# Moving the second batch's tap mixing from all four blocks of the first batch's convolution to the last three

## The reference

```python
logits = (x @ Wl.T + bl).reshape(Bq, Tq, H, K)
w = softmax(where(valid, logits, -inf), axis=-1)
y = einsum('bthk,btkhd->bthd', w, xg)
z = conv(y + bias, Wc) + bc
h = selu(z) @ W2.T + b2
```

## Time and profile before

| what | value |
|---|---|
| median of three runs | 1567.8 us (1564.4 to 1570.6) |
| the profiled execution, its own time | 1562.6 us |
| its span in the trace | 1560.8 us |
| TensorE (PE) busy | 1471.8 us, 94% |
| VectorE (DVE) busy | 1027.2 us, 66% |
| ScalarE (ACT) busy | 722.9 us, 46% |
| GpSimd (POOL) busy | 576.7 us, 37% |
| batch 0's convolution | from 48 to about 157 us of the span |

### The profile page before, as it was taken

How to read it: one execution, slowest core, us unless ns; L and a number is a source line. 1 busy time by engine, 2 the same in 40 slices (tenths; PEclk the granted TensorE clock), 3 DMA queues, 4 the chain that set the end, 5 groups by cost and what they waited for, 6 DMA issues and landing times.

```text
span 1560.8 us, 30456 instructions
## 1 busy us (share of the span) xinstructions
PE 1471.8 (94%) x11724; PEld 990.5 (63%) x11724; DVE 1027.2 (66%) x1973; ACT 722.9 (46%) x1272; POOL 576.7 (37%) x632
## 2 busy tenths in 40 slices
PE   2799999999999899999999999999999999999998
PEld 2456766766666677777777777778875444444444
DVE  2754434655566667677877787755647877876766
ACT  1331222122111255566655556557665665555654
POOL 2220001001101478603460237002995564555655
PEclk9999999999999999999999999999999999999999
DMA  7441110110000278703260225000233443344543
GB/s 192 111 130 31 24 35 18 31 34 21 22 21 28 71 159 187 172 2 63 62 164 6 64 62 136 6 20 2 84 90 111 120 142 110 120 137 117 151 129 107
DMA packets 143906, 128.47 MB, mean 82 GB/s; under 512 B 86970, under 2 KB 124306, under 8 KB 142738
## 3 DMA queue, kind: packets, MB, share of 16 engines
q1 hardware_dynamic: 127186, 110.65, 27.0%
q0 software_dynamic: 2272, 12.06, 2.5%
q10 hardware_dynamic: 14304, 3.81, 1.3%
HBM read 106.24 MB, written 5.28 MB: 71 GB/s over the span
## 4 chain that ended last, share of the span: by engine, by line
PE 66%; POOL 11%; DVE 9%; DMA 6%; ACT 3%; issue 2%; SPq 2%; POOLq 0%; DVEq 0%; ACTq 0%
PE ps L1729 6%; PE ps L1731 5%; PE ps L1730 5%; PE ps L1995 5%; PE ps L1996 5%; PE ps L1997 5%; PE ps L1937 3%; PE ps L1931 3%; PE ps L1932 3%; DMA region_k<-region_c 3%; PE ps L1866 3%; PE ps L1901 2%; PE ps L1890 2%; PE ps L1896 2%; PE ps L1891 2%; PE ps L2007 2%
## 5 line engine op out<-in xcount | busy, mean ns | idle before, releaser
L992 ACT ACTIVATE region_c<-ps 128x720 f16<-128x720 f32 (+1 forms) x228 | 175.3, 769 | 232.8 <-PE ps L1901 232.8
L859 POOL TENSOR_TENSOR region_k<-region_c,region_k 128x480 f16<-128x480 f32 x198 | 216.8, 1096 | 164.8 <-ACT region_k L1113 164.6
L1353 DVE TENSOR_TENSOR region_c<-ps,region_c 128x720 f16<-128x720 f32 (+1 forms) x228 | 205.9, 903 | 96.8 <-ACT ps L993 94.6
L1729 PE MATMUL ps<-region_k 128*128 128x360 f16 (+1 forms) x752 | 240.7, 320 | 2.7 <-DVE region_k L1182 2.7
L1730 PE MATMUL ps<-region_k 128*128 128x360 f16 (+1 forms) x752 | 239.8, 319 | 0.0
L1731 PE MATMUL ps<-region_k 128*128 128x360 f16 (+1 forms) x752 | 239.8, 319 | 0.0
L1358 DVE TENSOR_REDUCE region_c<-ps 120x1 f32<-120x512 f32 x252 | 173.3, 688 | 75.4 <-PE ps L1866 72.9
L1931 PE MATMUL ps<-region_k,region_c 128*120 128x129 f16 (+1 forms) x1368 | 179.0, 220 | 1.9 <-ACT region_c L992 1.9
L1932 PE MATMUL ps<-region_k,region_c 128*120 128x128 f16 (+1 forms) x1368 | 178.1, 219 | 0.0
L993 ACT ACTIVATE ps<-ps 128x720 f32<-128x720 f32 (+1 forms) x228 | 174.6, 766 | 0.0
L743 POOL TENSOR_TENSOR vare<-mv,eps 120x6 f32<-120x6 f32 x20 | 3.9, 197 | 452.0 <-DVE mv L1261 452.0
(11 more groups left out here) (275 smaller groups left out, 2725.0 us busy)
## 6 DMA issues: line engine op xcount, KB each, us to landing
gates<-gates_dram SPq DMA_DIRECT2D x384, 120.0 KB, 2.8
region_c<-in_k SPq DMA_DIRECT2D x56, 256.0 KB, 2.9
region_c<-in_v SPq DMA_DIRECT2D x56, 256.0 KB, 3.1
region_c<-in_WcT POOLq DMA_DIRECT2D x8, 1024.0 KB, 6.2
region_c<-in_experts SPq DMA_DIRECT2D x18, 352.0 KB, 3.0
gates<-band_dram SPq DMA_DIRECT2D x26, 189.0 KB
region_c<-in_k POOLq DMA_DIRECT2D x14, 256.0 KB, 3.0
region_k<-region_c SPq DMA_TRANSPOSE x120, 3.1
```

What stands on the lines that cost most here:

```text
L859: g.tensor_tensor(a_lo[u], ac[u], a_hi[u], ALU.subtract).then_inc(s["a_lo_ready"], 1)
L992: a.activation(halves(p_hi[u][0:parts]), st, ACT.Exp).then_inc(s["p_hi_ready"], 1)
L1353: v.tensor_tensor(halves(p_lo[u][0:parts]), two(2 * u, parts), halves(p_hi[u][0:parts]), ALU.subtract).then_inc(s["lo_ready"], 1)
L1729: mm(o, wh[:, m, j], xh[:, j:j + w], start=(j == 0), stop=False)
```

## The change

Batch 1's mixing, done during batch 0's convolution, is spread over quarters 12 to 45 and not 1 to 43. The mixing of batches 2 and 3, the attention steps and the weights' steps stay in their quarters.

```diff
-MIX_SPAN, ATTN_SPAN = (1, 43), (3, 48)
+MIX_SPAN, FIRST_SPAN, ATTN_SPAN = (1, 43), (12, 45), (3, 48)
...
-    for row, (first, last) in ((mix, MIX_SPAN), (down + attn, ATTN_SPAN)):
+    for row, (first, last) in ((mix, MIX_SPAN if b else FIRST_SPAN), (down + attn, ATTN_SPAN)):
```

## The result

In 21 runs each the changed kernel had a median of 1572.3 us and the kernel before 1569.4 us; the ratio is 1.0026 (95% interval 1.0017 to 1.0036), which is 4.1 us slower (2.7 to 5.6). The three estimates are 4.1, 6.9 and 3.9 us, on the mean 5.0 us or 0.3%; each interval lies clear of no change. The profiled execution took 1575.0 us, its span 1573.2.

What follows compares the result with a forecast made beforehand. TensorE was taken to bound the kernel; -9.0 + 9.6 + 3.1 + 3.9 = +7.6 us on the profiled 1562.6 gives 1570.2, and 5.2 more for the median gives 1575.4 us, range 1565 to 1580.

Steps and rivals of the forecast that it cites:

- what the prediction put at nothing: Split moved to quarter 43, batch 2's x load, weights' steps, second band write, later windows' reads: no cost to TensorE.
- What the change takes away: Batch 0's convolution: wait at logits 1 (3.1), slow clock behind it (3.1), old band 0 wait (2.8) go; 9.0 us.
- The walk to taps 1: VectorE's moved chain from quarter 12 at 71.6 us through logits, low 4 and sums 4, ending taps 1 at 91.8.
- rival 3: VectorE, relieved of backlog, has taps 1 ready by 82.2, so no band 0 wait: -5.1 us, 1562.7; chance 0.08.
- The hold in line 1155: In logits 1, GpSimd's addition set off by low 4 holds this VectorE instruction, 2.65 us over its usual 0.28.
- The wait at band 0: TensorE at quarter 21 waits 9.6 us for the band's 10.5 us way through DRAM after taps 1; bounds 7.8 to 10.9.
- rival 4: Piece 7's load shares DMA engines with band write and reads, 3 us more: wait 13, sum +11, 1579; chance 0.06.
- The slow clock behind it: After the long band 0 wait the granted clock drops, costing TensorE 3.1 us; ends 2 and 3.5.
- The short waits: Bank 3, TensorE waiting for VectorE's apply reads: band 4 2.6, band 1 1.1, apply 5 0.2; sum 3.9 us.
- The sum: Whole kernel: -9.0 + 9.6 + 3.1 + 3.9 = +7.6 us, 0.48% slower; terms' ends +3.3 to +10.4.
- What a measurement can tell: Whole-kernel timing: about 0.5% (7.8 us) is what a measurement can tell from no change.

Runs made afterwards that it cites:

- Experiment 4: Changed kernel with batch 1's eight band windows packed from quarter 25 to 42: ratio to before 0.9961; the same with logits and taps back at 1, 2, 4, 6: 0.9972.
- experiment 2: Kernel before, with logits 1 of batch 1 put into free bank 5 so TensorE need not wait there: ratio 0.9991.
- experiment 6: Changed kernel, high 5 behind taps 1, low 4, sums 4, low 5 in quarter 20: ratio 1.0014; with apply 0 and 3 earlier 0.9984; with late windows 0.9970.
- second and third comparison: The unedited changed kernel timed twice more against the kernel before: ratios 1.0044 and 1.0025.
- experiments 5: Changed kernel with low 4, sums 4 and high 5 moved behind taps 1, quarter 16: ratio to before 1.0035; with apply 0 and 3 one quarter earlier 0.9996.

## Why the prediction was right, and where it was too large

- **Direction and mechanism: right.** The change made the kernel slower, by a wait at band 0 that takes the place of two smaller ones. Experiment 4 shows it from the other side: give the transport four more quarters and the loss turns into a gain. No other wait of TensorE shows in the changed kernel between 47 and 180 us, save those counted below, so what the prediction put at nothing cost nothing.
- **What the change takes away (9.0 us): right as a count of what the profile held.** Both waits are gone in the profiles. But it was read as TensorE's own loss, and experiment 2 shows that it was VectorE's: a wait taken from logits 1 comes back at the product reads. The late place of the logits did relieve VectorE, so the 9 us went in the changed kernel; experiment 4 puts the worth of that move, once the windows are late, at 1.7 us only, net of the 2.5 us that late logits still left at band 0.
- **The walk to taps 1: right to 0.1 us once its start is allowed for.** Forecast 91.8 with quarter 12 at 71.6; measured 89.95, in an execution that started 1.4 us earlier and had its full clock sooner, with logits 0 read from 73.97 where 75.8 was forecast: both are 1.8 earlier. VectorE was not just in time for logits 0, as forecast, but idle for 1.24 us ahead of it; that changed nothing, since TensorE set the start. (In rival 3 the four pieces of VectorE's work called 7.8 us add up to 7.0 by the durations given; nothing hangs on it.) The hold in line 1155 was forecast at 2.93 and was 2.93. By the Trainium skill's rule (SBUF — State Buffer, "SBUF: two separate sides") this instruction, begun at 79.60 and so 0.42 us ahead of the addition at 80.02, would have got through; the trace again doesn't agree for that instruction.
- **The wait at band 0 (9.6 us): 11.7, 9.9 and 10.2.** The two last are within 0.6, partly by luck: the write was quicker than the 7.17 assumed and the read slower. The write took 8.4 us in the first profile and 6.0 and 6.3 in the others, having 5.4 to 8.5. Piece 7's load was issued 2.6 us behind it in all three, so the load doesn't explain the 8.4, and nothing here does. The read took 3.6, 4.2 and 4.2 us where the earlier trace rows had 2.76; that load was still under way beside it, and experiment 6 shows what loads beside the read cost. So rival 4, given 0.06, was in part a feature of every execution and not a case of its own, but the whole way was only 0.3 to 2.1 us longer than 10.5, not 3.
- **The slow clock behind it (3.1 us): about right in the profiles, and incomplete.** Take away the waits and the slow clock, and the stretch of before is 110.8 - 9.0 = 101.8. The changed kernel's three stretches less their waits are 105.3, 105.6 and 103.4: 3.5, 3.8 and 1.6 us of slow clock. In the first two it fell a second time, behind band 4's wait of 2.6 us, which I hadn't foreseen, since 2.8 us had not brought it down before; in the third the same wait left it at 1.00.
- **The short waits (1.1, 2.6, 0.2): 1.19, 2.59 and none.**
- **The sum: too large.** +7.6 us against +4.1 (2.7 to 5.6), 0.48% against 0.26%; the mean of the three comparisons is 5.0. The terms don't show an error of that size: the profiles' stretches grew by 6.4 to 10.7 us, their mean by 8.6. For the other kernels the stretch and the timed difference agree within 2.1 us (the table); for the changed kernel alone the timed difference is 1.8 to 6.3 us below the profiled one. Two figures on record narrow this. The whole spans of the three profiles average 1567.9 us, those of the two of before 1561.5: 6.5 more, and 2.1 less than the stretches say, because what lies ahead of the stretch and behind it happened to be shorter. And the timed runs' mean granted clocks tell how long each was at the lower level from the convolution on (the clock's shortfall from 1, times two, times the span, less 37.5 us where the record also holds the slow start ahead of the convolution): in the second and third comparison 25 and 23 us on the mean for the changed kernel, 24 and 23 for the one before, where the profiles have 29 and 24. At 0.37 us each, the price found behind the stretch, those 4 us more in the profiles are worth about 1.5 us, an estimate that would bring 6.5 to 5.0. So the slow clock is the term the record points at; the waits of the timed runs were not seen, and which term was smaller in them stays open.
- **What a measurement can tell (0.5%): too coarse.** The comparison of 21 runs has an interval of 0.0010 on either side and told 0.26% from no change.

## What to carry to other kernels

When a chain across engines and DRAM is moved in an instruction order written by hand, count the distance in time between its last producer and its first consumer, with all that stands between them on the slowest engine; a uniform respread of the row shrinks exactly that distance. A wait seen on the busiest engine need not be that engine's loss: give it its resource and see whether the wait returns elsewhere. And keep a consumer that shares a buffer with the bound engine off the places where the reader has a long piece of work first; here, one quarter earlier for two steps was worth 2.8, 6.1 and 4.7 us in three kernels.

## What the runs showed of the hardware

- One 1 MB load issued beside a band write of 124-byte rows, and another beside the reads that follow it, stretched that way through DRAM from 10 to 16 us, in two kernels with and two without them (experiments 5 and 6). The queues differ (ScalarE's and SyncE's for the band, GpSimd's for the load), and still the loads slow the band; the reads bear most of it.
- Waits of nearly equal length had different consequences for the clock. The granted clock was 0.50 behind 3.12 us of idling, 0.56 behind 2.59, 0.51 from 1.2 us behind 2.36 (experiment 6), and 1.00 behind 2.8 and behind 2.59 in the changed kernel's third profile. So each of these waits was a possible double cost for the schedule.
- The same program at nearly the same point (557 to 562 us) ran at a granted clock of 0.66 in one execution and 1.00 in another, with nothing changed. The time at the lower level behind the stretch, 8.6 to 21.9 us in fourteen profiles, goes with most of the 6 us by which that part's time spreads.
- A VectorE operation with one SBUF tensor as input (and one value per partition), line 1210 on 128 x 360 values, was held beside GpSimd's addition too: 2.69 us in the changed kernel's block 0, where an addition of 2.36 us began at 64.76, for its usual 0.41:

```profile
64.65 2.69 DVE L1210 TENSOR_SCALAR region_c<-region_c,bc_sb 128x360 f32<-128x360 f32 x1
```
